# Two-layer conditioned attention network: the causal mask of layer 1's rotary attention moved from TensorE to VectorE in chunks 2 to 6

## The reference, cut to what matters

```python
q = (xn @ Wq).reshape(b, n, h, dh).transpose(0, 2, 1, 3)
kv = xn @ Wkv
k, v = (kv[..., :dh], kv[..., dh:])
q = q * cos + _rotate_half(q) * sin
k = k * cos + _rotate_half(k) * sin
q = q * scale
sim = jnp.einsum('bhid,bjd->bhij', q, k)
causal = jnp.triu(jnp.ones((n, n), dtype=bool), k=1)
neg = -jnp.finfo(sim.dtype).max
sim = jnp.where(causal, neg, sim)
sim = sim - jax.lax.stop_gradient(jnp.max(sim, axis=-1, keepdims=True))
attn = jax.nn.softmax(sim, axis=-1)
out = jnp.einsum('bhij,bjd->bhid', attn, v)
```

## Time and profile before

| what | value |
|---|---|
| runs | 1327.89, 1330.05, 1330.46 us |
| median | 1330.05 us |
| profiled execution, its own time | 1327.77 us |
| its span, first to last instruction | 1325.9 us |
| PE / PEld / VectorE / ScalarE busy | 97% / 71% / 85% / 61% |
| clock granted to TensorE in the span | 1.000 of 2.4 GHz |

### The profile page before, as it was taken

One profiled execution on the slowest core, in us unless ns is written; L12 is line 12 of the kernel. 1 busy time (PEld: TensorE's weight loads), 2 busy tenths in 40 slices (PEclk: granted clock), 3 DMA queues, 4 the chain that ended last, 5 costly groups with the idle time before them and its releaser, 6 DMA issues.

```text
span 1325.9 us, 25724 instructions
## 1 busy us (share of the span) xinstructions
PE 1281.7 (97%) x9778; PEld 943.8 (71%) x9778; DVE 1129.5 (85%) x2921; ACT 809.4 (61%) x1592; POOL 85.1 (6%) x88
## 2 busy tenths in 40 slices
PE   5999999999999999999999889999999999999998
PEld 2444444688878888888887676667777878787867
DVE  4899999889989889898979798588888888879885
ACT  4999999874656565656555864644545554545323
POOL 0000000101020101011011000000000000000000
PEclk9999999999999999999999999999999999999999
DMA  9433343521202020202030320100000000000000
GB/s 378 141 72 80 80 104 87 171 79 49 63 11 80 2 81 1 81 1 81 11 123 27 149 63 11 41 1 17 1 25 1 25 2 23 9 9 9 9 1 24
DMA packets 26536, 73.69 MB, mean 56 GB/s; under 512 B 3992, under 2 KB 5156, under 8 KB 25136
## 3 DMA queue, kind: packets, MB, share of 16 engines
q1 hardware_dynamic: 25840, 71.10, 17.2%
q10 hardware_dynamic: 576, 0.98, 0.2%
HBM read 49.26 MB, written 22.81 MB: 54 GB/s over the span
## 4 chain that ended last, share of the span: by engine, by line
PE 57%; DVE 31%; ACT 8%; issue 3%; DMA 1%; SPq 0%; DVEq 0%; ACTq 0%
DVE work L1920 10%; PE psum L990 7%; PE psum L1021 6%; PE psum L599 6%; PE psum L766 4%; PE psum L1035 4%; PE psum L1063 4%; PE psum L646 3%; PE psum L570 2%; PE psum L579 2%; PE psum L1002 2%; PE psum L936 2%; DVE h_all L1920 2%; PE psum L698 1%; PE psum L1015 1%
## 5 line engine op out<-in xcount | busy, mean ns | idle before, releaser
L646 PE MATMUL psum<-h_all,w_big 128*128 128x256 f32 x1024 | 235.2, 382 | 1.3 <-ACT work L1353 1.2
L646 PEld LDWEIGHTS psum<-h_all,w_big 128*128 128x128 f32 x1024 | 190.0, 190 | 32.5 <-issue 5.7
L1920 DVE SCALAR_TENSOR_TENSOR work<-work,taps 128x240 f32<-128x240 f32 (+28 forms) x518 | 139.9, 344 | 0.0
L599 PE MATMUL psum<-w_big,h_all 128*64 128x512 f32 x512 | 121.1, 595 | 0.0
L990 PE MATMUL psum<-work,w_big 128*128 128x256 f32 x512 | 118.1, 379 | 0.5 <-DVE gru_mem L2533 0.5
L766 PE MATMUL psum<-w_big,gru_mem 128*128 128x256 f32 x512 | 113.7, 379 | 0.5 <-ACT gru_mem L1399 0.5
L1021 PE MATMUL psum<-w_big 128*128 128x256 f32 x448 | 105.4, 384 | 2.6 <-ACT w_big L1660 2.6
L766 PEld LDWEIGHTS psum<-w_big,gru_mem 128*128 128x128 f32 x512 | 96.9, 190 | 14.9 <-ACT gru_mem L1399 0.6
L990 PEld LDWEIGHTS psum<-work,w_big 128*128 128x128 f32 x512 | 96.0, 190 | 13.5 <-DVE gru_mem L2533 0.9
L1021 PEld LDWEIGHTS psum<-w_big 128*128 128x128 f32 x448 | 82.9, 190 | 22.0 <-issue 6.7
L2531 DVE TENSOR_TENSOR gru_mem<-psum,trig 128x256 f32<-128x256 f32 x128 | 53.7, 420 | 41.1 <-PE psum L990 37.0
(11 more groups left out here) (360 smaller groups left out, 2561.0 us busy)
## 6 DMA issues: line engine op xcount, KB each, us to landing
value_rows<-w_emb SPq DMA_DIRECT2D x128, 128.0 KB, 2.3
work<-value_rows SPq DMA_DIRECT2D x16, 1024.0 KB, 5.8
w_big<-in_Wq SPq DMA_DIRECT2D x2, 2048.0 KB, 16.8
w_big<-in_Wo SPq DMA_DIRECT2D x2, 2048.0 KB, 21.7
out<-w_big SPq DMA_DIRECT2D x15, 256.0 KB, 2.1
x_res<-out SPq DMA_DIRECT2D x15, 256.0 KB, 2.8
w_big<-in_Wv SPq DMA_DIRECT2D x1, 2048.0 KB, 18.0
w_big<-in_Wk SPq DMA_DIRECT2D x1, 2048.0 KB, 24.6
```

Of the source, the lines that this page charges most:

```text
L599: mm = pe.matmul(bank(4 + n)[j * B:(j + 1) * B, :], h_all[:, k, :, 2 * pair + j], w_big[:, 2, k * H * HD + n * 512:k * H * HD + (n + 1) * ...
L646: mm = pe.matmul(bank(n % 2)[:, o * TA:(o + 1) * TA], w_big[:, s, k * H * HD + at:k * H * HD + at + HD], h_all[:, k, bass.ds(i * BA, BA), ...
L1920: ins = dve.scalar_tensor_tensor(dst[:, :, lag:], src[:, :, :T - lag], tap, dst[:, :, lag:], ALU.mult, ALU.add)
```

## The change

A constant names chunks 2 to 6. In them rot_scores leaves out the four mask products of each group, and the first score product opens the sum in PSUM itself. In rot_soft_in, behind the transposition and ahead of the maximum, VectorE adds the mask (128 x 512, in place, the 32 mask columns repeated over the 16 heads) and waits for that addition. Chunks 0, 1 and 7 stay as they are.

```diff
+MASKED = range(2, NA - 1)
...
             def rot_scores(c, g):
                 pe.wait_ge(q_on.sem, H * c + H)
-                for b in range(GB):
+                added = c in MASKED
+                for b in range(0 if added else GB):
                     pe.matmul(bank(2 + g)[b * T:(b + 1) * T, :].rearrange("p (h i) -> p h i", h=H), mask_bf[:],
                               ident_bf[:, 0:T].unsqueeze(1).broadcast_to([P, H, T]), start=True, stop=False)
                 for s, q in ((0, q_cos), (1, q_sin)):
                     for b in range(GB):
                         tok = slice(g * P + b * T, g * P + (b + 1) * T)
                         mm = pe.matmul(bank(2 + g)[b * T:(b + 1) * T, :].rearrange("p (h i) -> p h i", h=H),
-                                       k_rot[:, s, tok], q[:, :, tok], start=False, stop=(s == 1))
+                                       k_rot[:, s, tok], q[:, :, tok], start=added and s == 0, stop=(s == 1))
                 mm.then_inc(sc_sum.sem, 1)
...
                 dve.transpose(att1.rearrange("p e j -> p (e j)"), bank(2 + g)).then_inc(st_on.sem, 1)
                 dve.wait_ge(st_on.sem, GA * c + g + 1)
+                if c in MASKED:
+                    link(dve.tensor_tensor(att1, att1, mask.unsqueeze(1).broadcast_to([P, H, T]), ALU.add))
                 rlink(dve.tensor_reduce(r_max, att1, AX.X, ALU.max))
                 dve.tensor_tensor(att1, att1, per_row(r_max, T), ALU.subtract).then_inc(z1_on.sem, 1)
```

## The result

The changed kernel takes 1337.18 us (median of 6 runs, 1336.05 to 1340.04); the kernel before, run beside it, 1329.65 (median of 6, 1327.89 to 1332.15). The ratio is 1.0051, with a 95% interval of 1.0039 to 1.0063: slower, by 6.8 us by the ratio and 7.5 between the medians. The forecast was 1334.2, 1330.5 to 1337.3.

The account below looks back on a forecast made before the run. TensorE was taken to set the pace, VectorE following. Additions delay VectorE's chain 1.23 us a chunk, less a 0.30 margin: 5 x 0.93 = 4.65 us slower, giving 1334.2 us, range 1330.5 to 1337.3 for 8 in 10.

Parts of the forecast that it names:

- the forecast's own 1331.5 to 1336: Whole kernel: the main case's range, from 3.7 to 5.8 us slower on the different base times; chance 0.73.
- the first rival: Chunks 2 to 6: VectorE is the bound or its delay is paid in full, 7.2 us, 1337.3; chance 0.10.
- The rule of the Trainium skill: Highest occupancy marks the bound, TensorE judged by weight loads (77%): VectorE at 85%, so 7.2 us in all.
- TensorE's share: Mask products in chunks 2 to 6: 0.43 us a chunk saved, about 0.3 to 0.4 left behind L960's wait for ScalarE.
- The addition: VectorE, each group of chunks 2 to 6: 0.69 us busy, 0.72 to the linked reduction; 1.44 a chunk.
- The walk: One chunk, VectorE results to TensorE's readers: group 0 0.51 us late, group 1 1.23, TensorE finally 0.93 late.
- the prediction's signs: Changed trace: five TensorE waits each before group 1's L1015 and before L970, in sum 1 us or more a chunk.
- The term that was mis-sized: TensorE's L970 after ScalarE's L1631: start 0.06 us after its end, so 0.93 late, 1.23 less a margin of 0.30.
- What is late next: VectorE's 0.74 us wait at L2504 takes the last 0.30 of its delay; nothing more is late.
- the bases of before: Whole kernel: 4.65 us added to the median (1334.7) and the mean (1333.7) of the kernel before; the middle, 1334.2, taken.
- the forecast's 4.65: Chunks 2 to 6: five chunks, each with a period 0.93 us longer.

Follow-up runs that it names:

- e9: The changed kernel with filler matmuls at the start and in chunk 7, and the order of chunks 2 to 6 rewritten: 1333.73 us.
- e10: e9 without the start fillers, and two projection tiles put ahead of group 0's value products in chunks 2 to 6: 1327.53 us, ratio 0.9979.
- e1: The changed kernel without VectorE's additions, so chunks 2 to 6 have no mask at all: 1329.46 us, ratio 0.9995.
- e2: The changed kernel with TensorE's mask products kept as well, so the mask counts twice in chunks 2 to 6: 1337.78 us, ratio 1.0053.
- e8: The changed kernel with filler matmuls at the start and in chunk 7, VectorE adding the mask in group 0 only, TensorE writing group 1's: 1335.53 us.
- e3: The change made in chunk 2 alone, against the kernel before: 1331.9 us, ratio 1.0016.
- e5: The changed kernel with 14 filler matmuls in chunk 7 and none at the start: 1335.14 us, ratio 1.0042.
- e11: The kernel before with 14 filler matmuls in chunk 7 and none at the start: 1329.76 us, ratio 0.9999.
- e12: e10 with the mask put back on TensorE in chunks 2 to 6 and no additions by VectorE: 1329.16 us, ratio 0.9990.
- e6: The kernel before with filler matmuls, 6 and 20 in the recurrence's first two steps and 14 in chunk 7: 1334.3 us.
- e13: e10 without the filler matmuls in chunk 7: 1327.97 us, ratio 0.9983.

## Why the prediction was right, and where it was not

- **The number.** The mechanism came out as forecast, the number only just. The median, 1337.18, lies 3.0 above the forecast of 1334.2, outside the forecast's own 1331.5 to 1336, and 0.1 inside the upper end of the range. That end was the price of the first rival (VectorE is the bound, 1337.3). That the median falls on it is a coincidence: 5.25 us from the chunks and some 2 from the clock. The periods tell the two apart, not the time: 65.33, where the forecast had 65.2 and the rival 65.7.
- **What bounds.** TensorE, with VectorE behind it. e9 and e10 show it: the same work in another order has a period of 64.30 or 63.76. The rule of the Trainium skill that was weighed (Perfetto Trace Analysis, Identifying the Most-Contended Engine) would have it 7.2 slower; chunks 2 to 6 are 5.25 slower, and e10, with every addition, 0.52 a chunk faster than before. So the waits were the better guide here.
- **TensorE's share.** 0.43 a chunk was predicted, of which 0.3 to 0.4 would be left behind L960; L1065 then comes 0.38 early (5.05 after the transposes, 5.43 before), and e1 shows 0.38. Group 0's scores reach VectorE 0.21 earlier, as predicted (L2543 starts 2.57 after the transposes, 2.78 before).
- **The addition.** 0.69 busy and 0.72 to 0.73 to the next start, as the layer 0 row said.
- **The walk**, relative to the transposes L953: group 0's back-transposition is 0.53 late (0.51 predicted). Group 0's L1017 starts 0.38 early and still ends late, since its fourth sequence's weights wait 0.26 for L2543 inside the row (958.99 above): the L1065 behind it starts 0.16 late (0.16). Group 1's back-transposition is 1.26 late (1.23), L1017 of group 1 0.77 (0.75), L2500 1.26 (1.23), L971 1.05 (0.93). The five waits on each line are there, but they make 0.74 a chunk, where the prediction's signs asked for 1 or more. That sign contradicted its own walk, by which some 0.6 and 0.2 us are waited in the open, and the rest of the delay uses up TensorE's lead or lies inside the busy row. In e2 and e8 the same walk, with the margins read from the changed kernel, gives the measured periods.
- **The term that was mis-sized** is the last: L971 comes 0.14 behind ScalarE's end (969.16 to 969.30 in the chain), where the prediction took 0.06 from a VectorE release of another line. These 0.08 and the 0.03 more on VectorE's chain make the 0.12 a chunk, to the rounding; 0.6 us in all.
- **What is late next.** The margin at L2504 (now L2506) went from 0.74 to 0.54, where 0.44 was foreseen; it holds, nothing runs into the next chunk, and e3 shows the same.
- **What was not in the sum** is TensorE's clock in chunk 7, 1.3 us in the profiles and some 2 between the medians, and that the changed kernel's six runs are all at a clock that low. This is the step that put the sum's result on the bases of before: it took the scatter of those runs for noise that the change would share. With the clock alike, the forecast's 4.65 stands against 5.4 (e5 less e11), and against 7.5 without that.

## What to carry to other kernels

Work moved from a bounding engine to one with gaps costs what the receiving chain's margins don't cover: walk from each added instruction to the first wait of the bounding engine, and take the release time from the very line that will wait. Then ask whether the order can be changed so that the lengthened chain has margin, since here that turned a loss of 5 us into a gain of 2.5 with the same work (0.7 of it is the new order's own, which the unchanged mask gets too). And look inside rows that count as busy: a matmul group that is longer than its twin (1.68 against 1.14) holds a wait. Where a difference is under 0.3%, put the runs side by side at equal granted clock, and the periods of the changed part beside the medians.

## What the runs showed of the hardware

- **Three levels of one kernel's time.** The 78 runs of the kernel before that stood beside the experiments fall into groups by the granted clock of the span: 7 at 1.000 (median 1327.9), 53 at 0.999 (1330.0) and 17 at 0.996 (1332.0), one between. The profiles of the other kernels say what takes a run off 1.000. Those at 0.999 have one drop: e5's, e10's and e12's at 25 to 27 us, e6's to e8's at 287. Those of the changed kernel, e1, e3 and e13, at 0.997, have that at 25 us and one in chunk 7. e2's, at 0.996, has a longer drop at the start (0.84, 0.50 and 0.98 in the windows of 5 us from 20 on) and that in chunk 7. No execution of the kernel before below 1.000 was profiled, so which drops its 17 runs at 0.996 have isn't shown. Its one profile (1327.77) is at 1.000; so the comparison of two profiles held 3.1 us that the change doesn't explain. A ratio of medians holds less of it, but not none.
- **Which kernel drops in chunk 7 is open.** TensorE pauses 1.69 us ahead of L1023 there in the changed kernel and 1.70 ahead of L1021 in the kernel before, and the products behind it take 5.41 in the one and 3.72 in the other. Of the changed kernel's runs all six are at 0.995 to 0.997, of e1's and e3's ten of eleven each, of e13's four of eleven, of the kernel before's 18 of 78 at 0.997 or less. The Trainium skill (TensorE: Matmul & The Clock Gate, The HAM clock gate) says that the activity is watched in free-running windows and that the result varies from run to run; the scatter agrees with that, but that it varies with the kernel no rule or run explains. With fourteen fillers in the pause the changed kernel has one of five runs at 0.997 (e5) and no profile with them has the drop, but the fillers don't rule it out: two of e10's eleven runs are at 0.997, three each of e11's and e12's at 0.997 or less. For the kernel before, three of eleven (e11) against 18 of 78 show no gain.
- **Fillers can cost far away, and move a drop.** 26 matmuls in the first 25 us kept the clock at 1.00 there; the drop came at 287 us instead, behind a pause of 1.90, and the kernel became 4 us slower, in waits of TensorE at 286 us and behind. That it waited for its instructions there is argued, not shown.
- **A change of tile shape seems to cost 0.14.** e10's period lies 0.14 under e1's, with the same products and the same few waits. In e10 L971 (tiles of 128 x 32) follows L1017 (32 x 128) directly, and in e1 whole-array products stand between them, one return to the whole array more. The Trainium skill (TensorEngine Tiling (Array Packing), Key Properties) says that a change of mode drains the engine; the 0.11 by which group 0's mask stage was longer than group 1's is of the same size. e12 and the kernel before differ by the same 0.14 (64.14 and 64.28). No run changes the shapes alone, so this is an estimate.
